# Layer 1's foreign-position mask: from an addition on VectorE to an 8-row matmul on TensorE

## The chip, the cores and the metric

The kernel runs on one core of one Trainium2 chip. Its engines are TensorE (PE, with its weight loads as PEld), VectorE (DVE), ScalarE (ACT), GpSimd (POOL) and SyncE (SP), which issues DMAs. The metric is device time in microseconds; the median of several runs is compared.

## What is computed

The reference is a two-layer transformer on x of shape [4, 512, 256]. The change lies in layer 1's attention, which attends over the first axis of 4, for each of 512 positions by itself:

```python
def _L1_attn_ref(x, w_qkv, w_proj):                 # x: (s=4, b=512, 256)
    s, b, _ = x.shape
    qkv = jnp.einsum('sbh,ph->sbp', x, w_qkv)
    ...                                             # 16 query heads, 4 key/value heads, head size 128
    scores = jnp.einsum('bhsd,bhtd->bhst', q, k) * scale
    attn = jax.nn.softmax(scores, axis=-1)          # over t, four values
    out = jnp.einsum('bhst,bhtd->bhsd', attn, v)
    ...
    return jnp.einsum('sbe,he->sbh', out, w_proj)

x = x + _L0_attn_ref(_layernorm(x), ...)
x = x + _L0_ffn_ref(_layernorm(x), ...)
x = x + _L1_attn_ref(_layernorm(x), L1_attn_w_qkv, L1_attn_w_proj)
x = x + _L1_ffn_ref(_layernorm(x), ...)
```

So each position has, for each head, a 4 x 4 matrix of scores.

## The kernel before

Four stages follow each other, one for each line above. In stage 3, `layer1_attention`, the 512 positions are split in G = 4 rounds of 128. A round's 512 rows of X (4 sequence items times 128 positions) are normalised, transposed on TensorE (`turn`), and multiplied by the weights into 20 tiles of queries and keys (`queries_keys`, 16 query heads and 4 keys, 128x512 each). ScalarE rounds a tile to bf16 (`qk_hi`), and VectorE makes the rest (`qk_lo`); all products are formed as high*high + high*low + low*high.

`scores` takes the round in NB = 4 blocks j, one PSUM bank each. A block holds four groups of 8 positions. The 8 positions and 4 sequence items of a group are the 32 keys of one column tile of TensorE, and the same 32 are the queries, for all heads. Of the 32 x 32 products of a head only those between equal positions are wanted: 4 of 32 in a row. The others, those of foreign positions, get a mask of -1e30. Before the change VectorE does it: `softmax_a(g, j)` transposes the bank in 32x32 blocks to SBUF, adds `mask` (128x32, broadcast over the heads), takes the maximum over the 8 positions (which leaves one value for each of the 4 items), then the maximum of the four, and subtracts. ScalarE takes the exponential, and `softmax_b` sums, inverts, multiplies, spreads the four weights over 32 columns with `same` (128x8, 1 at equal positions), and transposes back. `outputs` multiplies with the values, `project` applies the output projection and adds to X.

The orders are written out by hand and are the same for each round. TensorE: values(g), turn(g+1), five chunks of four tiles of queries_keys(g+1) with outputs(g, 0) to (g, 3) behind the first four chunks, project(g, 0), scores(g+1), project(g, 1). VectorE: normalised and x_low for g+1; then phases with softmax_b(g, 0) and softmax_a(g, 2); softmax_b(g, 1), outputs_lo(g, 0) and softmax_a(g, 3); softmax_b(g, 2) and outputs_lo(g, 1); and so on, each followed by three decoding steps for the weights of stage 4 and mixed evenly with four qk_lo (`interleave`, which spreads extra steps over a given number of main steps); at the end add(g, 0), softmax_a(g+1, 0) and (g+1, 1), add(g, 1). ScalarE: qk_hi of a chunk, outputs_hi, an exponential. In the last round there are no tiles to be made.

GpSimd first builds `mask` (16 dependent affine_selects, lines 1345 to 1349) and `same` (line 1352), and after them computes rstd of the layer norm (lines 1355, 1357), for which `normalised(0)` waits. Later it turns decoded 4-bit weights into bf16 pairs: line 154 (multiplication by scales), 157 (cast), 159 (rest), released by the last decoding step on VectorE, line 141.

Lines in the rows below: 1370 all three-product matmuls, 1381 the transposes `turn`, 1419 scores, 1436 outputs; on VectorE 1536 to 1551 softmax_a (1539 is the mask's addition), 1557 to 1575 softmax_b, 1582 outputs_lo, 1589 qk_lo, 1606 normalised, 1631 the addition to X; on ScalarE 1484 qk_hi, 1490 the value copies, 1496 the exponential, 1502 outputs_hi.

## Time and profile before

| what | value |
|---|---|
| median of 3 runs | 1284.75 us (1284.47 to 1284.92) |
| the profiled execution | 1279.96 us |
| its span | 1278.20 us |
| mean granted TensorE clock | 0.894 |
| TensorE matmuls busy | 1028.5 us, 80% |
| VectorE busy | 871.9 us, 68% |
| ScalarE busy | 499.3 us, 39% |
| GpSimd busy | 334.7 us, 26% |

Stage 3 runs from 642.8 us to about 985 us of the span. Its rounds 0 to 2 are nearly alike, 81 us each; the last is shorter. In the timeline a row gives start, duration, engine, line, operation, output<-inputs, and in square brackets how long the engine had been idle before and what ended that. Durations on TensorE contain the passage through the array, and the rows of neighbouring matmuls overlap: the distance from start to start is the pace. A row with xN merges N instructions.

### The profile page before, as it was taken

To read this page: it belongs to the slowest core of one execution; us is meant where nothing else is said; L and a number is where in the kernel's file an instruction comes from. 1 tells how busy PE (TensorE), PEld (TensorE's weight loads), DVE (VectorE), ACT (ScalarE), POOL (GpSimd) and SP (SyncE) were. 2 spreads that over 40 slices of the span, in tenths; PEclk is the share of its full clock that TensorE was granted. 3 is DMA by queue.
4 is the path that set the end of the run, shared out by engine and by line. 5 is a ranking of instruction groups with operands and counts; after the bars stand their busy time and mean duration, and the time that the engine had idled before them with its cause. 6 is when DMAs were issued, how large, how long until landed. Compare 5 with 4: busy or idle time off the path is not lost. (4 is left out here: it accounts for less than half of the span.)

```text
span 1278.2 us, 20287 instructions
## 1 busy us (share of the span) xinstructions
PE 1028.5 (80%) x6960; PEld 592.4 (46%) x6960; DVE 871.9 (68%) x1548; ACT 499.3 (39%) x972; POOL 334.7 (26%) x347
## 2 busy tenths in 40 slices
PE   2898888965859679497358998989968799999996
PEld 1444444533435345253124464464647355556553
DVE  4776667623789989989855845627572587777764
ACT  1144444442645544546323413414220244444442
POOL 2042424252343425342410311302131350000000
PEclk9698999997879789698669899898988899999998
DMA  6422121101001001001000000100000110000001
GB/s 172 93 76 84 54 92 47 51 3 39 1 1 41 1 1 41 0 1 42 1 16 2 26 10 9 25 2 18 15 17 1 41 27 1 1 1 0 1 1 66
DMA packets 37017, 35.78 MB, mean 28 GB/s; under 512 B 8520, under 2 KB 33352, under 8 KB 36944
## 3 DMA queue, kind: packets, MB, share of 16 engines
q1 hardware_dynamic: 35664, 33.79, 9.6%
q10 hardware_dynamic: 1280, 1.05, 0.6%
q8 instruction: 42, 0.69, 0.2%
q14 instruction: 31, 0.25, 0.1%
HBM read 27.28 MB, written 6.29 MB: 26 GB/s over the span
## 5 line engine op out<-in xcount | busy, mean ns | idle before, releaser
L779 DVE TENSOR_REDUCE bm<-ps 128x4 f32<-128x512 f32 x160 | 106.2, 685 | 36.5 <-PE ps L549 32.0
L696 ACT ACTIVATE pt<-ps 128x1024 f32<-128x1024 f32 (+1 forms) x96 | 82.3, 881 | 79.3 <-PE ps L603 78.0
L967 POOL TENSOR_TENSOR wt<-lg,mid 128x2048 f32<-128x2048 f32 x16 | 74.7, 4670 | 84.2 <-DVE mid L1186 84.2
L993 PE MATMUL ps<-stage,ones 128*128 128x512 bf16 x128 | 52.5, 410 | 54.7 <-DVE xr_lo L1152 26.3
L545 PE MATMUL ps<-ks,qs 96*128 96x512 bf16 (+3 forms) x256 | 71.3, 324 | 22.4 <-DVE bm L779 8.6
L1589 DVE TENSOR_TENSOR qk_lo<-ps,qk_hi 128x512 bf16<-128x512 f32 x80 | 54.8, 685 | 42.2 <-ACT qk_hi L1484 41.7
L1801 ACT ACTIVATE g<-ps 128x512 f32<-128x512 f32 x64 | 38.2, 597 | 111.9 <-PE ps L1748 111.9
L1851 DVE SCALAR_TENSOR_TENSOR g<-g,ps 128x512 f32<-128x512 f32 x64 | 43.9, 686 | 53.8 <-ACT g L1801 53.5
L493 POOL TENSOR_SCALAR_AFFINE_SELECT pt<-pt 128x256 f32<-128x256 f32 (+1 forms) x96 | 45.9, 482 | 128.4 <-ACT pt L696 128.0
L1209 DVE SCALAR_TENSOR_TENSOR X<-ps,cw,X 128x256 f32<-128x256 f32 (+1 forms) x128 | 61.9, 484 | 23.0 <-PE ps L997 14.8
L1763 PE MATMUL ps<-ew_hi,it_hi 128*128 128x256 bf16 x256 | 70.0, 273 | 7.8 <-DVE it_lo L1867 5.1
L1484 ACT ACTIVATE qk_hi<-ps 128x512 bf16<-128x512 f32 x80 | 47.8, 598 | 72.6 <-PE ps L1370 72.6
L1370 PE MATMUL ps<-xT_hi,wq_hi 128*128 128x512 bf16 x160 | 70.0, 437 | 7.7 <-DVE xT_lo L1612 5.0
L1370 PE MATMUL ps<-wp_hi,oT_hi 128*128 128x256 bf16 x256 | 71.0, 277 | 4.9 <-DVE oT_lo L1582 4.9
L154 POOL TENSOR_TENSOR mag_gu<-stage 128x512 f32<-128x512 fp8e4 x16 | 17.6, 1098 | 214.8 <-DVE stage L141 214.8
L1098 ACT ACTIVATE far<-far 128x256 f32<-128x256 f32 x128 | 51.4, 406 | 50.4 <-DVE far L1198 50.4
L1370 PE MATMUL ps<-wp_lo,oT_hi 128*128 128x256 bf16 x256 | 71.0, 277 | 0.0
L1370 PE MATMUL ps<-wp_hi,oT_lo 128*128 128x256 bf16 x256 | 71.0, 277 | 0.0
L1763 PE MATMUL ps<-ew_hi,it_lo 128*128 128x256 bf16 x256 | 70.0, 273 | 0.0
L1763 PE MATMUL ps<-ew_lo,it_hi 128*128 128x256 bf16 x256 | 69.9, 273 | 0.0
L1370 PE MATMUL ps<-xT_lo,wq_hi 128*128 128x512 bf16 x160 | 69.4, 434 | 0.0
L1370 PE MATMUL ps<-xT_hi,wq_lo 128*128 128x512 bf16 x160 | 68.6, 429 | 0.0
(228 smaller groups left out, 2826.1 us busy)
## 6 DMA issues: line engine op xcount, KB each, us to landing
qs<-scratch_q SPq DMA_DIRECT2D x64, 64.0 KB, 2.6
ks<-scratch_k SPq DMA_DIRECT2D x48, 64.0 KB, 2.5
q_next<-in_w_qkv SPq DMA_DIRECT2D x4, 768.0 KB, 4.8
X<-in_x SPq DMA_DIRECT2D x4, 512.0 KB, 7.0
w_next<-in_router_w SPq DMA_DIRECT2D x4, 512.0 KB, 4.1
w_next<-in_expert_w SPq DMA_DIRECT2D x4, 512.0 KB, 5.0
p_next<-in_w_proj SPq DMA_DIRECT2D x4, 512.0 KB, 5.6
out<-X SPq DMA_DIRECT2D x4, 512.0 KB, 4.7
```

The source lines that it names most:

```text
L493: pool.affine_select(out=t, in_=t, compare_op=ALU.is_ge, fill=0.0, base=0, pattern=[[0, len(heads)], [1, P]], channel_multiplier=-1).then_ ...
L545: pe.matmul(ps[:, o + P * i:o + P * (i + w)], qs[0:SHIFT, h, P * j:P * (j + 1)], ks[0:SHIFT, h, P * k0:P * (k0 + w)], start=(i == 0), stop ...
L696: act.activation(pt[kt][:, heads[0]:heads[-1] + 1, :], src, ACT.Exp).then_inc(s_exp, 1)
L779: ins = dve.tensor_reduce(bm[:, 2 * g + i // 5, 4 * (i % 5):4 * (i % 5) + 4], src.rearrange("p (k q) -> p k q", k=4), AX_X, ALU.max)
L967: pool.tensor_tensor(wt[:, :, :], lg[t % 2][:, :, :], over_experts(mid), ALU.subtract).then_inc(s_mid, 1)
L993: pe.matmul(out, ones4[:, :], bias, start=True, stop=False)
L1098: act.activation(far[:, e, :], far[:, e, :], ACT.Copy, accum_out=cw[t % 2][:, e:e + 1]).then_inc(s_cw, 1)
L1209: dve.scalar_tensor_tensor(x, bank(4 + u, D, D * e), c_t[:, 2 * u + e:2 * u + e + 1], x, ALU.mult, ALU.add).then_inc(s_c, 1)
L1370: mm = pe.matmul(out, lhs[a](c), rhs[b_](c), start=(n == 0), stop=(n == 3 * chunks - 1), **kw)
L1484: act.activation(qk_hi[:, m // (HQ + 1), m % (HQ + 1), :], bank(QK_BANK[m]), ACT.Copy).then_inc(s_qkhi, 1)
L1589: dve.tensor_tensor(qk_lo[:, k, h, :], bank(QK_BANK[m]), qk_hi[:, k, h, :], ALU.subtract).then_inc(s_qklo, 1)
L1763: mm = pe.matmul(bank(6 + t // 2, D, D * (t % 2)), a[m % 2][:, P * t:P * (t + 1)], w[2][:, m % 2, D * (m // 2):D * (m // 2 + 1)], start=(m ...
```

## The change

The mask goes into PSUM ahead of the scores. For each bank j, TensorE first issues one matmul of spread8 (8 rows x 128, bf16, 1 where column mod 8 is the row) with apart (8 rows x 512, bf16, 0 where column mod 8 is the row and -1e30 elsewhere), over the full bank, with start=True. The scores of the bank are then added with start=False. There are 4 such matmuls in a scores call, 16 in all. VectorE's addition is gone in each of the 16 softmax_a, whose steps are 4 instead of 5, and the counts of `interleave` follow. GpSimd builds `same` directly (128x8 instead of 128x32), and apart and spread8 from it, still ahead of rstd. TensorE waits for both before scores(0).

```diff
-        SMA, SMB = 5, 5
-        TURNED, MASKED, PICKED, MAXED, SHIFTED = 1, 2, 3, 4, SMA
+        SMA, SMB = 4, 5
+        TURNED, PICKED, MAXED, SHIFTED = 1, 2, 3, SMA
...
-                pool.memset(mask[:, :], -1.0e30).then_inc(const, 1)
+                pool.memset(same[:, :], 0.0).then_inc(const, 1)
                 for m in range(P // 8):
                     pool.wait_ge(const, 2 + m)
-                    mk = mask[:, :].rearrange("p (b q) -> p b q", q=8)
-                    pool.affine_select(out=mk, in_=mk, compare_op=ALU.not_equal, fill=0.0, base=-8 * m,
-                                       pattern=[[0, 4], [-1, 8]], channel_multiplier=1).then_inc(const, 1)
+                    pool.affine_select(out=same[:, :], in_=same[:, :], compare_op=ALU.not_equal, fill=1.0, base=-8 * m,
+                                       pattern=[[-1, 8]], channel_multiplier=1).then_inc(const, 1)
                 pool.wait_ge(const, 2 + P // 8)
-                pool.tensor_scalar(same[:, :], mask[:, 0:8], 0.0, None, ALU.is_ge).then_inc(const, 1)
+                pool.tensor_scalar(apart[:, :].rearrange("p (n q) -> p n q", q=8),
+                                   same[:, :].rearrange("p (o q) -> p o q", o=1).to_broadcast([P, BANK // 8, 8]),
+                                   1.0e30, -1.0e30, ALU.mult, ALU.add).then_inc(const, 1)
+                pool.tensor_copy(spread8[0:8, :].rearrange("p (n q) -> p n q", q=8),
+                                 same[0:8, :].rearrange("p (o q) -> p o q", o=1).to_broadcast([8, P // 8, 8])
+                                 ).then_inc(const, 1)
...
                     for j in range(NB):
+                        pe.matmul(bank(j), spread8[0:8, :], apart[0:8, :], start=True, stop=False, skip_group_check=True)
                         for k in range(KV):
...
-                                        start=(i == 0), stop=(i == 2), skip_group_check=True)
+                                        start=False, stop=(i == 2), skip_group_check=True)
...
+                pe.wait_ge(const, 4 + P // 8)
                 scores(0)
...
-                    dve.tensor_tensor(s[:, :, :], s[:, :, :],
-                                      mask[:, :].rearrange("p (o q) -> p o q", o=1).to_broadcast([P, H1, T8]),
-                                      ALU.add).then_inc(s_sma, 1)
-                    yield
-                    dve.wait_ge(s_sma, SMA * n + MASKED)
```

On GpSimd, at the head of stage 3, there stood before:

```order
L1344 MEMSET half 128x16
L1345 MEMSET mask 128x32
L1349 AFFINE_SELECT mask<-mask 128x32 x16
L1352 TENSOR_SCALAR same<-mask 128x8
L1355 TENSOR_SCALAR rstd<-mv 128x4
L1357 TENSOR_TENSOR rstd<-rstd,half 128x4
```

and now:

```order
L1345 MEMSET half 128x16
L1346 MEMSET same 128x8
L1349 AFFINE_SELECT same<-same 128x8 x16
L1352 TENSOR_SCALAR apart<-same 128x512
L1355 CAST spread<-same 8x128
L1360 TENSOR_SCALAR rstd<-mv 128x4
L1362 TENSOR_TENSOR rstd<-rstd,half 128x4
```

One operation more, of 512 columns, stands ahead of rstd.

On TensorE, at the start of scores(0), behind the last tile of queries and keys, there stood before:

```order
L1370 MATMUL ps<-xT_hi,wq_hi 128x512
L1370 MATMUL ps<-xT_lo,wq_hi 128x512
L1370 MATMUL ps<-xT_hi,wq_lo 128x512
L1419 MATMUL ps<-qk_hi 32x128 x4
L1419 MATMUL ps<-qk_lo,qk_hi 32x128 x4
L1419 MATMUL ps<-qk_hi,qk_lo 32x128 x4
```

and now:

```order
L1375 MATMUL ps<-xT_hi,wq_hi 128x512
L1375 MATMUL ps<-xT_lo,wq_hi 128x512
L1375 MATMUL ps<-xT_hi,wq_lo 128x512
L1420 MATMUL ps<-apart,spread 128x512
L1425 MATMUL ps<-qk_hi 32x128 x4
L1425 MATMUL ps<-qk_lo,qk_hi 32x128 x4
L1425 MATMUL ps<-qk_hi,qk_lo 32x128 x4
```

The mask matmul stands ahead of the twelve fours of its bank; at banks 1 to 3 it has fours on both sides.

On VectorE, in the first phase of a round, from softmax_a(g, 2) to the decoding steps (stage) and the first step of softmax_b(g, 1), with the tiles (qk_lo) between them, there stood before:

```order
L1536 STREAM_TRANSPOSE ew_hi<-ps 128x512 [waits softmax1,sc1]
L1539 TENSOR_TENSOR ew_hi<-ew_hi,mask 128x512 [waits shifted1]
L1589 TENSOR_TENSOR qk_lo<-ps,qk_hi 128x512 [waits qk1hi]
L1544 TENSOR_REDUCE four<-ew_hi 128x64 [waits shifted1]
L1548 TENSOR_REDUCE mx_0<-four 128x16 [waits shifted1]
L1551 TENSOR_TENSOR four<-four,mx_0 128x64 [waits shifted1]
L1589 TENSOR_TENSOR qk_lo<-ps,qk_hi 128x512 [waits qk1hi]
L135 TENSOR_SCALAR stage<-stage 128x64 [waits gathered_gu]
L138 TENSOR_SCALAR stage<-stage 128x128 [waits decoded_gu]
L141 SCALAR_TENSOR_TENSOR stage<-stage 128x128 [waits decoded_gu]
L1557 TENSOR_REDUCE sm_1<-four 128x16 [waits exp1]
L1589 TENSOR_TENSOR qk_lo<-ps,qk_hi 128x512 [waits qk1hi]
```

and now:

```order
L1543 STREAM_TRANSPOSE ew_hi<-ps 128x512 [waits softmax1,sc1]
L1546 TENSOR_REDUCE four<-ew_hi 128x64 [waits shifted1]
L1591 TENSOR_TENSOR qk_lo<-ps,qk_hi 128x512 [waits qk1hi]
L1550 TENSOR_REDUCE mx_0<-four 128x16 [waits shifted1]
L1553 TENSOR_TENSOR four<-four,mx_0 128x64 [waits shifted1]
L135 TENSOR_SCALAR stage<-stage 128x64 [waits gathered_gu]
L1591 TENSOR_TENSOR qk_lo<-ps,qk_hi 128x512 [waits qk1hi]
L138 TENSOR_SCALAR stage<-stage 128x128 [waits decoded_gu]
L141 SCALAR_TENSOR_TENSOR stage<-stage 128x128 [waits decoded_gu]
L1559 TENSOR_REDUCE sm_1<-four 128x16 [waits exp1]
L1591 TENSOR_TENSOR qk_lo<-ps,qk_hi 128x512 [waits qk1hi]
```

The addition is gone, the tiles stand at the same step numbers and so one step of the softmax later, and the last tile shown (tile 4) keeps its place behind L1557's step.

## Rows read from the trace of the kernel before

**Rows 1.** Waits, 680 to 965 us: engine line <- waited for: total us, times, longest.

```profile
DVE X L1631 <- PE ps L1370: 53.6, 6, 10.2
...
PE ps L1436 <- DVE oT_lo L1582: 18.1, 12, 5.3
```

**Rows 2.** Groups of instructions: the mask's addition, busy us, mean ns of one.

```profile
L1539 DVE TENSOR_TENSOR ew_hi<-ew_hi,mask 128x512 f32<-128x512 f32 x8 | 5.5, 693 | 0.3
```

**Rows 3.** Timeline, VectorE, the border between rounds 0 and 1.

```profile
771.36 0.69 DVE L1631 TENSOR_TENSOR X<-ps,X 128x512 f32<-128x512 f32 x1 [8.50 <-PE ps L1370]
```

**Rows 4.** Timeline, TensorE: the end of scores(1), and a change of shape in round 1.

```profile
760.44 0.24 PE L1419 MATMUL ps<-qk_lo,qk_hi 128*32 128x128 bf16 x4
760.50 0.24 PE L1419 MATMUL ps<-qk_hi,qk_lo 128*32 128x128 bf16 x4
760.67 0.28 PE L1370 MATMUL ps<-wp_hi,oT_hi 128*128 128x256 bf16 x1
...
786.57 0.38 PE L1370 MATMUL ps<-xT_lo,wq_hi 128*128 128x512 bf16 x1
786.79 0.38 PE L1370 MATMUL ps<-xT_hi,wq_lo 128*128 128x512 bf16 x1
787.10 0.39 PE L1436 MATMUL ps<-ew_hi,v 32*128 32x128 f32 x4
```

**Rows 5.** Timeline, GpSimd and VectorE, the start of stage 3.

```profile
647.80 0.25 POOL L1352 TENSOR_SCALAR same<-mask 128x8 f32<-128x8 f32 x1
...
649.49 1.38 DVE L1606 TENSOR_SCALAR xn<-X,mv,rstd 128x256 f32<-128x256 f32 x4 [4.95 <-POOL rstd L1357]
```

**Rows 6.** Groups of instructions on GpSimd, by form: busy us, mean ns of one.

```profile
L949 POOL TENSOR_SCALAR ties<-identb 128x128 bf16<-128x128 bf16 x8 | 4.2, 530 | 0.6
...
L1349 POOL TENSOR_SCALAR_AFFINE_SELECT mask<-mask 128x32 f32<-128x32 f32 x16 | 3.7, 229 | 1.1
...
L457 POOL CAST b_part<-b_next 2x512 bf16<-2x512 f32 x4 | 2.4, 599 | 0.0
...
L1935 POOL TENSOR_SCALAR_AFFINE_SELECT ident<-ident 128x128 f32<-128x128 f32 x1 | 0.3, 292 | 0.2 <-POOL ident L1933 0.2
```

**Rows 7.** Timeline, TensorE, values(0), turn(1), the first tile, and turn(2).

```profile
692.47 0.38 PE L1370 MATMUL ps<-wq_hi,xT_lo 128*128 128x512 bf16 x1
695.33 1.07 PE L1381 MATMUL ps<-ident,xn 128*128 128x128 f32 x8 [2.49 <-ACT v L1490]
698.02 0.59 PE L1370 MATMUL ps<-xT_hi,wq_hi 128*128 128x512 bf16 x1 [1.62 <-ACT xT_hi L1477]
...
778.25 1.06 PE L1381 MATMUL ps<-ident,xn 128*128 128x128 f32 x8 [0.78 <-ACT v L1490]
```

**Rows 8.** Timeline, ScalarE and VectorE, round 0, tile 4.

```profile
708.56 1.24 ACT L1484 ACTIVATE qk_hi<-ps 128x512 bf16<-128x512 f32 x2
...
709.21 0.69 DVE L1589 TENSOR_TENSOR qk_lo<-ps,qk_hi 128x512 bf16<-128x512 f32 x1
```

**Rows 9.** Timeline, VectorE and GpSimd, round 0, tiles 8 and 9.

```profile
720.27 0.69 DVE L1589 TENSOR_TENSOR qk_lo<-ps,qk_hi 128x512 bf16<-128x512 f32 x1 [1.00 <-ACT qk_hi L1484]
...
721.16 0.23 DVE L1563 TENSOR_TENSOR four<-four,sm 128x64 f32<-128x64 f32 x1
...
721.42 0.69 DVE L1567 TENSOR_TENSOR ew_hi<-four,same 128x512 f32<-128x512 f32 x1
721.47 1.65 POOL L159 TENSOR_TENSOR up_lo<-mag_gu,up_hi 128x512 bf16<-128x512 f32 x1 [0.18 <-POOL up_hi L157]
...
722.45 0.69 DVE L1589 TENSOR_TENSOR qk_lo<-ps,qk_hi 128x512 bf16<-128x512 f32 x1 [0.34 <-ACT qk_hi L1484]
```

**Rows 10.** Timeline, GpSimd and VectorE, the last round.

```profile
940.83 1.10 POOL L154 TENSOR_TENSOR mag_gu<-stage 128x512 f32<-128x512 fp8e4 x1 [34.51 <-DVE stage L141]
941.00 1.00 DVE L1563 TENSOR_TENSOR four<-four,sm 128x64 f32<-128x64 f32 x1
...
943.38 1.15 POOL L159 TENSOR_TENSOR gate_lo<-mag_gu,gate_hi 128x512 bf16<-128x512 f32 x1 [0.18 <-POOL gate_hi L157]
```

More of the change, by code:

```diff
@@ L1266, in layer1_attention @@
         v = st.sb("v1", [P, NB, KV, HD1], F32)
-        mask = st.sb("mask1", [P, T8], F32)
         same = st.sb("same1", [P, 8], F32)
+        apart = st.sb("apart1", [P, H1 // KV * T8 * KV], BF16)
+        spread8 = st.sb("spread8", [P, P], BF16)
         mx = [st.sb(f"mx1_{n}", [P, H1], F32) for n in range(2)]
@@ L1621, in _ @@
                 x_low(0)
-                dve.wait_ge(const, 3 + P // 8)
+                dve.wait_ge(const, 2 + P // 8)
                 interleave(queries_keys_low(0), NM, chain(statistics(1), statistics(2), statistics(3)), 6 * B)
```

## The prediction

> **What bounds the kernel now.** I read three views of layer 1's attention, in this order: the waits of its stretch, the timeline of a border between two rounds, and the timeline inside a round. In the waits the reader is to see that each engine waits for the other. VectorE waits 53.6 us for TensorE before the additions to X; TensorE waits 18.1 us for VectorE before the attention outputs, inside the rounds [rows 1]. So the path changes engine by place, and the change has to be weighed place by place. It takes 16 additions of 0.69 us from VectorE (8 on ew_hi [rows 2], 8 alike on ew_lo), 0.73 each with the gap, and gives TensorE 16 matmuls.
>
> **The three borders between rounds.** Two of a round's additions stand here, in softmax_a(g+1, 0) and (g+1, 1). Behind them VectorE idles 8.50 us until project(g, 1) is done [rows 3]; they are hidden, and taking them away gains 0. TensorE has no slack: project(g, 0), scores(g+1) and project(g, 1) follow without a gap, and X, the values and the next transposes hang on the last of them. What scores(g+1) grows by is paid in full.
>
> No 8-row matmul stands in the trace, so its price comes from neighbours. A 512-column matmul followed by one of another array shape leads to the next start 0.31 us later (786.79 to 787.10), against 0.22 in the same shape (786.57 to 786.79) [rows 4]. The column-tiled 128*32 matmuls run in fours, 0.06 us from four to four, but the first full-width one starts 0.17 behind the last four (760.50 to 760.67) [rows 4]: going from them into the mask matmul costs 0.11 more. At banks 1 to 3 that makes 0.31 + 0.11 = 0.42 us; at bank 0 the change of shape on the way in is paid today already, so 0.31. One scores call grows by 0.31 + 3 x 0.42 = 1.57 us, the three borders by **4.7 us**. Lower bound: 12 x 0.22 = 2.6. Upper bound, nothing overlaps: the 0.24 of a four's own row less its 0.06, and the 0.38 of a 512-column row [rows 4], 0.56 each, 12 x 0.56 = 6.7. I take 0.42 and 0.31, since both parts are measured changes of shape in this stage.
>
> The Trainium skill, TensorEngine Tiling (Array Packing), Key Properties, says that changing the tiling mode drains TensorE. This speaks against the change, since the mask matmul is put between column-tiled ones, two changes a bank. A full drain would make the borders 6.7 instead of 4.7. The trace agrees only in part: the full-width matmul starts 0.17 us after the four's start, while the four's row lasts 0.24 [rows 4].
>
> **The start of the stage.** GpSimd builds its constants before rstd, and VectorE waits 4.95 us for that rstd [rows 5], with TensorE behind. GpSimd's order is the path. Its 16 affine_selects shrink from 32 to 8 columns: 0.229 at 32 and 0.292 at 128 [rows 6] are 0.66 ns a column, so 16 x 24 columns save 0.25. The comparison of 0.25 (128x8) goes [rows 5], and the copy spread8 (8x128) comes; I take it at the same 0.25. The tensor_scalar apart has 512 columns: 0.53 at 128 [rows 6] and 0.25 at 8 [rows 5] are 2.33 ns a column, so 1.42. Sum -0.25 - 0.25 + 0.25 + 1.42 = **+1.2 us**, all on the path. Lower bound: the 512-column cast's 0.60 instead of 1.42 [rows 6], +0.4. I take 1.42, by the rows of the same operation.
>
> **Round 0.** scores(0) grows by 1.57 too. But turn(1) now starts at 695.33, 2.49 us after the values' end, behind ScalarE's four value copies [rows 7]; those come behind exp(0, 1), which waits for softmax_a(0, 1). Two additions less bring them forward by 1.46, and then the end of the values decides: 692.47 + 0.38 + 1.57 = 694.42, and the transposes 0.78 behind, as in round 1 (778.25) [rows 7], at 695.20: **-0.1 us**. The wait before turn(1) falls from 2.49 to 0.8, which may spare half-rate matmuls after it; I count nothing for that (rival e).
>
> **Inside rounds 0 to 2.** Two additions each, in softmax_a(g, 2) and (g, 3). The first is followed by three decode steps, a step of softmax_b and then qk_lo of tile 4. This starts at 709.21, right behind ScalarE's qk_hi of it (708.56, two rows of 0.62, the first done near 709.2) [rows 8]. ScalarE is late because outputs_hi(g, 0) stands ahead in its queue, and that hangs on TensorE. VectorE arrives 0.8 us earlier and waits 0.8 longer. Behind the second addition VectorE already waits 1.00 us for tile 8 at 720.27 [rows 9]. Gain in six places: 0; what is late next is ScalarE, behind TensorE.
>
> There is a loss. VectorE's multiplication L1563 lasts 0.23 us [rows 9], but 1.00 where GpSimd's L154 runs: it then ends 0.07 after L154's 941.93 [rows 10]. Two operations that both read two SBUF tensors do not overlap here. GpSimd's chain L154, L157, L159 is released by the decode steps. In phase 2 these move 0.7 us forward, while L1563 stays at 721.16, behind tile 8. L159 now starts at 721.47 behind L1567's 721.42 and lasts 1.65 [rows 9]; moved to 720.75 it goes first and takes its usual 1.15 [rows 10], until 721.90. L1563 then ends at 721.98 and L1567 at 722.70, 0.6 later than now. VectorE's wait of 0.34 us before tile 9 [rows 9] takes a part: tile 9 and the oT_lo behind it, for which TensorE waits, come 0.2 us later, and 0.3 and 0.4 in rounds 1 and 2, where I read that wait as 0.28 and 0.18. **+0.9 us** together. In phase 1 the same shift puts L1567 about 0.05 us ahead of L159; I count nothing.
>
> **The last round.** No tiles are made, and VectorE's queue is the path: TensorE's longest wait for it, 5.3 us [rows 1], is here. Both additions count, except that after the first oT_lo meets an oT_hi that is not ready: 0.54 + 0.73 = **-1.3 us**.
>
> **Sum.** 4.7 + 1.2 - 0.1 + 0.9 - 1.3 = +5.4 us. The profiled execution took 1279.96 us (span 1278.20 and 1.76 around it): 1285.4. It lies 4.8 below the median of the timed runs, and nothing shown says where; I assume the same offset after the change and add the difference to the median: 1284.75 + 5.4 = **1290.1 us**, +0.42%.
>
> **Rivals.**
> (a) Faster: VectorE is the path inside the rounds after all, six additions of 0.73 pay -4.4 in place of the +0.9, and the mask matmuls cost 0.22. Sum 2.6 + 1.2 - 0.1 - 4.4 - 1.3 = -2.0, 1282.7; it stays below the time before up to 0.38 us a mask matmul. For it: the 18.1 us of waits [rows 1]. Against: each addition is followed by a VectorE wait for ScalarE.
> (b) The additions to both queues are cheap, 0.22 a matmul and 0.4 at the start: 2.6 + 0.4 - 0.1 + 0.9 - 1.3 = +2.5, 1287.2. For it: no row has an 8-row operand. Against: the changes of shape in rows 4.
> (c) Full drain: 6.7 in place of 4.7, +7.4, 1292.1.
> (d) In phase 1 L159 comes first and L1567 waits 1.1 us for it, in three rounds: +8.7, 1293.5. For it: a margin of 0.05. Against: VectorE won with the same margin at 721.42 [rows 9].
> (e) TensorE's clock. At 698.02 a 512-column matmul takes 0.59 us instead of 0.38 [rows 7], the pace of 1.2 instead of 2.4 GHz, after TensorE had idled. Five such matmuls more or fewer are 1.1 us of either sign. This widens the cases and is none by itself.
>
> **Chances.** Forecast 0.55, (a) 0.07, (b) 0.18, (c) 0.10, (d) 0.10. A measurement can tell about 0.2% (2.6 us) from no change. Slower by more: 0.76 (forecast, c, d, a little of b); within: 0.19 (most of b, a part of a); faster: 0.05, with a clock gain on (a). The range leaves out (a) and the upper part of (d): from 1285.8, (b) with a clock gain, to 1294.5, (d) with a clock loss.
>
> **What would show it.** From the first matmul of scores(g+1) to project(g, 1): 1.6 us more. The operation apart at 1.4 us on GpSimd and rstd 1.2 later. VectorE's wait before tile 8 at 1.7 instead of 1.0 us, with tile 8 as far behind ScalarE as now. L1563 of phase 3 at 0.8 instead of 0.23. The last round's final outputs nearer to its values by 1.3. The forecast is wrong if tiles 4 and 8 follow VectorE's step before them without a wait, or if a mask matmul takes under 0.3 us from start to start.

## The result

Each of the two kernels was timed 12 times: 1283.61 us median before and 1286.22 us after, a ratio of 1.0029 with a 95% interval of 1.0015 to 1.0042. The ratio compares the means; the medians lie 2.6 us apart, the means 3.7 us. The change makes the kernel slower, by about 3.7 us. Timed a second time, beside other runs of the kernel before, the same kernel stood at 1.0042 (1.0026 to 1.0058), 5.4 us (after_again below). The forecast was +5.4 us, +0.42%.

The profiled execution of the kernel after took 1288.49 us, its span 1286.8 us, 8.6 more than the span before. Not all of this is the change: in this trace stage 3 starts at 647.74 us instead of 642.78, before any changed instruction has run. In the second profile of the same kernel it starts at 642.60. So the stage is compared from its own start on.

The first view of the profile after is the busy time of the engines.

```profile
PE 1036.8 (81%) x6976; PEld 599.3 (47%) x6976; DVE 862.3 (67%) x1532; ACT 499.7 (39%) x972; POOL 334.4 (26%) x348
```

16 matmuls more on PE, 16 instructions less on DVE (1532 against 1548) and 9.6 us less busy there. These answer to [rows 1], waits of stage 3 from 680 us to its end (engine line <- waited for: total us, times, longest):

```profile
DVE X L1633 <- PE ps L1375: 60.9, 6, 10.4
...
PE ps L1442 <- DVE oT_lo L1584: 20.4, 16, 4.2
```

VectorE waits 7.3 us longer for TensorE at the borders, and TensorE's wait for oT_lo has not fallen (20.4 against 18.1), though VectorE has less to do. Two things lengthen the wait at the borders: the additions that used to fill a part of it are gone, and scores last longer. How much is due to which was not separated.

The window view gives a stretch's start and end, its length, the busy time of PE, PEld, DVE, ACT and POOL (with counts), the granted TensorE clock and the DMA's share. Three stretches of the kernel before: stage start to the first transposes, scores at the second border, outputs(3, 0) to project of the last round.

```profile
642.78:650.93 8.15, 0.00 (x0) 0.00 (x0) 3.11 (x12) 0.00 (x0) 5.31 (x21) 0.50 0.31 60
838.62:841.41 2.79, 2.79 (x193) 2.69 (x193) 2.42 (x4) 0.00 (x0) 0.00 (x0) 1.00 0.02 6
941.04:965.31 24.27, 11.65 (x129) 9.61 (x129) 21.83 (x43) 8.53 (x18) 13.73 (x15) 0.61 0.10 23
```

The same of the kernel after:

```profile
647.74:657.23 9.49, 0.00 (x1) 0.01 (x1) 3.11 (x12) 0.00 (x0) 5.38 (x22) 0.50 0.24 55
843.74:848.14 4.40, 4.40 (x197) 3.08 (x196) 3.63 (x7) 0.26 (x1) 0.00 (x0) 1.00 0.01 4
950.51:973.56 23.05, 12.09 (x128) 10.04 (x129) 20.54 (x42) 8.54 (x18) 13.03 (x15) 0.60 0.09 24
```

Three terms of the forecast can be read off: the start is 1.34 longer (forecast 1.2), a scores call 1.61 (1.57), the last round 1.22 shorter (1.3). What lies between is less plain, and most experiments are about it.

### The profile page after: what moved, and what is told of

The parts are those of the page before. It is cut to its first block and busy times, and to the rows that moved or that the text cites. A ratio compares the mean times of both kernels' runs of the same rounds, so it can differ in the third digit from the quotient of the medians.

```text
span 1286.8 us, 20309 instructions
## 1 busy us (share of the span) xinstructions
PE 1036.8 (81%) x6976; PEld 599.3 (47%) x6976; DVE 862.3 (67%) x1532; ACT 499.7 (39%) x972; POOL 334.4 (26%) x348
## 3 DMA queue, kind: packets, MB, share of 16 engines
q10 hardware_dynamic: 1280, 1.05, 0.6%
## 5 line engine op out<-in xcount | busy, mean ns | idle before, releaser
L154 POOL TENSOR_TENSOR mag_gu<-stage 128x512 f32<-128x512 fp8e4 x16 | 17.6, 1099 | 217.5 <-DVE stage L141 217.5
L1375 PE MATMUL ps<-xT_hi,wq_hi 128*128 128x512 bf16 x160 | 66.9, 418 | 8.2 <-DVE xT_lo L1614 5.0
L995 PE MATMUL ps<-rw_hi,xr_hi 128*128 128x512 f32 x128 | 69.6, 544 | 0.0
L1375 PE MATMUL ps<-xT_lo,wq_hi 128*128 128x512 bf16 x160 | 66.1, 413 | 0.0
```

The lines of the kernel that those rows point to most:

```text
L995: pe.matmul(out, x_hi(c), w_hi[:, c, cols], start=False, stop=False)
L1375: mm = pe.matmul(out, lhs[a](c), rhs[b_](c), start=(n == 0), stop=(n == 3 * chunks - 1), **kw)
```

## The experiments

All ratios are to the kernel before, timed on the same chip. A profile of each kernel was taken too. mask_128 and wide_select were timed once each, for their profiles; they have no ratio.

### The two halves of the change, one at a time

The first kernel takes the additions away and puts nothing in their place. Its output is not the reference's.

```diff
-                    dve.tensor_tensor(s[:, :, :], s[:, :, :],
-                                      mask[:, :].rearrange("p (o q) -> p o q", o=1).to_broadcast([P, H1, T8]),
-                                      ALU.add).then_inc(s_sma, 1)
```

> The kernel before without its 16 additions and with no mask matmul: layer 1's foreign positions are not masked out, a part of the computation is left out. It shows what the additions were worth to the kernel before, with scores and start unchanged. Theory of the prediction: the last round 1.3, round 0's start about 1.6 less what the values' end leaves of it, inside the rounds nothing or a loss of 0.9: 1 to 2.5 us faster than the kernel before. Rival, VectorE as the path inside: 1.3 + 1.5 + 4.4 = 7 us faster.

The second keeps both, the mask matmuls and the additions; its small constant for them is made after rstd.

```diff
+                    if n == 0:
+                        pool.tensor_scalar(mask[:, :].rearrange("p (n q) -> p n q", q=8),
+                                           same[:, :].rearrange("p (o q) -> p o q", o=1).to_broadcast([P, T8 // 8, 8]),
+                                           1.0e30, -1.0e30, ALU.mult, ALU.add).then_inc(const, 1)
...
+                    dve.tensor_tensor(s[:, :, :], s[:, :, :],
+                                      mask[:, :].rearrange("p (o q) -> p o q", o=1).to_broadcast([P, H1, T8]),
+                                      ALU.add).then_inc(s_sma, 1)
```

> The changed kernel with VectorE's 16 additions kept as well (the mask is then put on twice); their 128x32 mask is built by GpSimd after round 0's rstd. It shows what the additions are worth where the matmuls are there. Theory of the prediction: only the last round's two count, 1.3 us, and the 0.9 us of collisions inside the rounds go away: 0.4 us slower than the changed kernel, 1286.6. Rival, VectorE as the path inside the rounds: 6 x 0.73 + 1.3 = 5.7 us slower, 1292. In between, if the second addition of a round counts wherever TensorE runs at full rate (as in rounds 0 and 1 of the changed kernel's profile): 0.7 to 0.9 for each such round, 2 to 3.5 us slower.

| | no mask matmuls | mask matmuls |
|---|---|---|
| with additions | 1 (before) | 1.0039 (1.0024 to 1.0055) |
| without additions | 0.9988 (0.9967 to 1.0010) | 1.0029 and 1.0042 (after, twice) |

Read along the lower row, mask matmuls and their constants cost 0.41 to 0.54%, 5 to 7 us; the terms of the forecast on that side (borders 4.7, start 1.2, scores(0) 1.57) make 7.5. Read down the columns, the additions are worth 0.12% without mask matmuls, and -0.03 or +0.10% with them: 1.5 us at most by the middle values, with intervals of 0.15 to 0.2% to either side, so not told apart from nothing. Sixteen additions of 0.73 us are 11.7 us of VectorE's time. Most of it was hidden, or given back elsewhere.

The traces say where they count. The last round is 23.05 us in no_mask and 24.29 in keep_add: 1.2 us, as forecast. The other place is round 0: from scores(0) to turn(1) no_mask takes 9.19 us, where before takes 10.63. The two additions are worth 1.44 us there, as the forecast had it (1.46), and the four mask matmuls of scores(0) use that up. What they do inside the rounds is told below.

### The matmul itself: its rows, and its place

One kernel makes it 128 rows tall, with zeros in the other 120 rows of `spread8`.

```diff
-                        pe.matmul(bank(j), spread8[0:8, :], apart[0:8, :], start=True, stop=False, skip_group_check=True)
+                        pe.matmul(bank(j), spread8[:, :], apart[:, :], start=True, stop=False, skip_group_check=True)
```

> The changed kernel with the mask matmul over all 128 rows (rows 8 to 127 of spread8 are zero): twelve times the contraction rows, the same 512 columns, and at bank 0 no change of shape on the way in. If the price is that of columns and of the change from and to the column-tiled fours, the distance from one mask matmul of a call to the next stays at 1.10 us. If the few rows are what makes it dear or cheap, it moves. One memset more at the start, 0.2 to 0.3 us.

Another puts the four mask matmuls together ahead of the call's scores, so that there is one change of shape in place of seven.

```diff
                     for j in range(NB):
                         pe.matmul(bank(j), spread8[0:8, :], apart[0:8, :], start=True, stop=False, skip_group_check=True)
+                    for j in range(NB):
                         for k in range(KV):
```

> The changed kernel, with the four mask matmuls of a scores call issued together ahead of all the scores, so that the array's shape changes once instead of four times. If about half of a mask matmul's 0.43 us is the change of shape, the four cost 0.22 each and one change of 0.1: a scores call falls from 4.70 us (761.87 to 766.57) to about 4.0, and the three borders by 2 us together, 1284.3. If the 512 columns with 8 rows are dear in themselves, the call stays at 4.6 to 4.7.

The second border in the window view, first of mask_128, then of masks_first:

```profile
839.25:843.67 4.42, 4.42 (x198) 3.01 (x196) 3.66 (x7) 0.26 (x1) 0.00 (x0) 1.00 0.01 4
```

```profile
844.40:848.16 3.76, 3.76 (x198) 2.98 (x197) 2.38 (x5) 0.00 (x0) 0.00 (x0) 1.00 0.02 4
```

120 rows more (16 times the rows; the expectation's "twelve times" is a slip) cost 0.02 us a call, nothing. The order does count: without a mask a call takes 2.79, with the four together 3.76, with them apart 4.40. So the columns of the four cost 0.97, about 0.24 each, and the changes of shape between the banks 0.64, 0.21 for each of the three banks. The forecast had 0.22 and 0.20 (0.31 + 0.11 - 0.22).

The timeline of the kernel after shows it matmul by matmul:

```profile
762.81 0.23 PE L1425 MATMUL ps<-qk_hi,qk_lo 128*32 128x128 bf16 x4
762.97 0.38 PE L1420 MATMUL ps<-apart,spread 8*128 8x512 bf16 x1
763.29 0.24 PE L1425 MATMUL ps<-qk_hi 128*32 128x128 bf16 x4
...
764.07 0.39 PE L1420 MATMUL ps<-apart,spread 8*128 8x512 bf16 x1
764.39 0.24 PE L1425 MATMUL ps<-qk_hi 128*32 128x128 bf16 x4
```

From the last four to the mask matmul 0.16 us (0.06 without a change), from it to the next four 0.32 (0.22). Sum above the pace of fours: 0.42, the number of the forecast. A full drain would have cost 0.56 by the lengths of the rows; here neither change waits for the 0.23 or 0.38 us that its forerunner's row lasts (the profile models the ends of these rows, so this compares with modelled ends).

In the time of the kernel the better order shows nothing: 1.0039 (1.0024 to 1.0053) for masks_first, beside 1.0029 and 1.0042. Two borders save 0.64 each, but the first of that profile has a stall, "[1.46 <-issue]" 0.6 us before the call's end, told of below, and the interior of round 0 came out long (43.08 us, at a granted clock of 0.80). A gain of some 2 us in 1280 isn't settled by these runs.

### GpSimd's constants, off the path

GpSimd builds the constants between the first rstd and the second instead of ahead of both. In the kernel after (`apart` and `spread8` move with the selects):

```diff
-                pool.memset(same[:, :], 0.0).then_inc(const, 1)
-                for m in range(P // 8):
...
                 for n, rows in enumerate((slice(0, 1), slice(1, G))):
+                    if n == 1:
+                        pool.memset(same[:, :], 0.0).then_inc(const, 1)
+                        for m in range(P // 8):
...
                     wait_alone(pool, s_mv, B * rows.stop, passed_pool)
```

> The changed kernel, with GpSimd's 16 affine_selects, apart and spread8 moved behind round 0's rstd. In the changed kernel rstd starts 6.6 us after the stage's first GpSimd instruction and VectorE waits 6.28 us for it, though its statistics end 1.7 us after that instruction. If GpSimd's order is the path at the stage's start, VectorE's wait falls to about 1.5 us (0.2 + 0.2 + 1.04 of rstd), the kernel is 4.8 us faster than the changed one, about 1281.5, and 1 to 2 us faster than the kernel before; the constants are ready long before scores(0). If something else stands behind (a weight or a DMA), the gain is under 1 us.

The stage reaches its first transposes 4.88 us after its start instead of 9.49, and the ratio falls from 1.0029 and 1.0042 to 1.0015 (0.9996 to 1.0033). That is 1.8 to 3.5 us by the middle values, less than the 4.6 us saved at the start, and the kernel did not come out faster than the kernel before, as had been expected. The part of the forecast on round 0 can be read here without a half-rate stretch: scores(0) to turn(1), before and in this kernel.

```profile
684.70:695.33 10.63, 8.15 (x216) 4.98 (x217) 6.31 (x15) 2.98 (x7) 2.90 (x3) 1.00 0.01 2
```

```profile
679.88:690.40 10.52, 9.74 (x220) 5.35 (x221) 4.90 (x12) 3.11 (x7) 2.91 (x3) 1.00 0.01 2
```

-0.11 us, with PE 1.59 us busier: the two additions less pay for the four matmuls more, as the forecast had it (-0.1).

The same move in the kernel before, with its `mask` and `same`:

> The kernel before with mask and same built behind round 0's rstd, VectorE's additions kept, no mask matmul. If GpSimd's order is the path at the stage's start there as well, the stretch from the stage's first GpSimd instruction to the first transposes falls from 8.15 to 4.9 us and nothing else moves: 3.3 us faster than the kernel before, ratio 0.9975, and faster than both kernels. If the earlier start is given back at the half rate of TensorE's clock, under 2 us.

It gave 0.9971 (0.9956 to 0.9987), 3.7 us less than before: faster than both kernels, and close to the 3.3 us expected. Its first transposes come 4.90 us after the stage's start instead of 8.15, and the whole stage, to the first transposes of the next, takes 348.64 us instead of 352.14. 

Late constants and mask matmuls together:

> The changed kernel with both edits: constants behind round 0's rstd, and the four mask matmuls of a scores call together. By sections against the kernel before: -3.3 at the start, three scores calls +0.96 each, the last round -1.2, round 0 -0.1, inside the rounds -0.6 to +0.9 each: -1.7 us at the middle, ratio 0.9987. If it isn't below 1.000, something that the sections don't show takes the gain.

0.9985 (0.9969 to 1.0000), between the two and near the 0.9987 expected; its scores call takes 3.76 us at the second border, as in masks_first. With the constants out of the way, the mask on VectorE is still the better place than the mask matmuls of the change: 0.9971 against 1.0015 for late_const, with intervals that do not meet. Against the grouped ones (0.9985) the intervals overlap, and the runs do not settle it.

### The start of the stage, by its parts

The timeline of GpSimd at the head of stage 3, before, and after:

```profile
643.03 4.68 POOL L1349 TENSOR_SCALAR_AFFINE_SELECT mask<-mask 128x32 f32<-128x32 f32 x16
```

```profile
648.04 5.24 POOL L1349 TENSOR_SCALAR_AFFINE_SELECT same<-same 128x8 f32<-128x8 f32 x16
653.37 0.62 POOL L1352 TENSOR_SCALAR apart<-same 128x512 bf16<-128x512 f32 x1
654.05 0.28 POOL L1355 CAST spread<-same 8x128 bf16<-8x128 f32 x1
```

The sum of the forecast was right (+1.2, measured +1.34), but two of its parts were wrong and cancelled out. The operation apart takes 0.62 and not 1.42. The 16 selects got longer, by 0.56, where they should have saved 0.25. One kernel makes the tile wide again:

```diff
-                    pool.affine_select(out=same[:, :], in_=same[:, :], compare_op=ALU.not_equal, fill=1.0, base=-8 * m,
-                                       pattern=[[-1, 8]], channel_multiplier=1).then_inc(const, 1)
+                    pool.affine_select(out=wd, in_=wd, compare_op=ALU.not_equal, fill=1.0, base=-8 * m,
+                                       pattern=[[0, 4], [-1, 8]], channel_multiplier=1).then_inc(const, 1)
```

> The kernel after, with the 16 affine_selects made over 128x32 again, as in the kernel before, and `same` taken from the first 8 columns; all else as after. If the time of a dependent step on GpSimd grows when the tile gets narrower (0.293 us at 32 columns against 0.328 at 8, as the two traces have it), the 16 selects take 4.7 us instead of 5.24 and the stage's first transposes come 0.5 us earlier. If instead the slower steps come from elsewhere (the order of the instructions around them, or the state of that run), they stay at 5.2.

```profile
645.61 5.85 POOL L1351 TENSOR_SCALAR_AFFINE_SELECT wide<-wide 128x32 f32<-128x32 f32 x16
```

The theory that narrower steps take longer fell: wide is slower still. But the groups by form tell more (busy us, mean ns of one | idle time just before them), here of the kernels before and after and of wide_select:

```profile
L1349 POOL TENSOR_SCALAR_AFFINE_SELECT mask<-mask 128x32 f32<-128x32 f32 x16 | 3.7, 229 | 1.1
```

```profile
L1349 POOL TENSOR_SCALAR_AFFINE_SELECT same<-same 128x8 f32<-128x8 f32 x16 | 3.1, 193 | 2.3
```

```profile
L1351 POOL TENSOR_SCALAR_AFFINE_SELECT wide<-wide 128x32 f32<-128x32 f32 x16 | 3.7, 231 | 2.3
```

The duration does go by the width (229 and 231 ns at 32 columns, 193 at 8); what doubled is the idle time between the steps, from 1.1 to 2.3 us, in both kernels that fill in 1.0 in place of 0.0. The last kernel goes back to starting from -1e30 and filling in 0.0, in the narrow tile, with a comparison behind it:

```diff
-                pool.memset(same[:, :], 0.0).then_inc(const, 1)
+                pool.memset(mask8[:, :], -1.0e30).then_inc(const, 1)
...
-                    pool.affine_select(out=same[:, :], in_=same[:, :], compare_op=ALU.not_equal, fill=1.0, base=-8 * m,
+                    pool.affine_select(out=mask8[:, :], in_=mask8[:, :], compare_op=ALU.not_equal, fill=0.0, base=-8 * m,
...
+                pool.tensor_scalar(same[:, :], mask8[:, :], 0.0, None, ALU.is_ge).then_inc(const, 1)
```

> The kernel after, but its 16 affine_selects start from -1e30 and fill in 0.0, as those of the kernel before do, in the narrow 128x8 tile; a comparison (0.25 us, as before) then makes `same` of it. The wide select, back at 128x32, still had the longer gap: there 16 take 5.85 us at 231 ns each, where the kernel before takes 4.68 at 229; in the kernel after, 5.24 at 193. Theory: the gap between dependent steps is 0.07 us with fill 0.0 and 0.14 with fill 1.0. Then the 16 take 16 x (0.193 + 0.07) = 4.2 us, the comparison gives back 0.25 to 0.35, and turn(0) comes 0.7 us earlier than in the kernel after: 8.8 instead of 9.49 us behind the stage's start. Rival: the gap comes from where the tile lies or from what stands around the selects; they stay at 5.2 us and turn(0) comes 0.3 us later. In the time of the kernel 0.7 us are 0.05%, at the edge of what the rounds can tell: expected ratio 1.003.

```profile
643.58 4.09 POOL L1350 TENSOR_SCALAR_AFFINE_SELECT mask<-mask 128x8 f32<-128x8 f32 x16
647.76 0.25 POOL L1353 TENSOR_SCALAR same<-mask 128x8 f32<-128x8 f32 x1
```

```profile
L1350 POOL TENSOR_SCALAR_AFFINE_SELECT mask<-mask 128x8 f32<-128x8 f32 x16 | 3.1, 192 | 1.1
```

4.09 us, and the idle time is 1.1 again. The fill value, or the value that stands in the tile, which was changed along with it, makes 0.07 us a step; which of the two was not tried. turn(0) comes 8.59 us after the stage's start instead of 9.49. The time of the kernel doesn't show the 0.9: 1.0039 (1.0023 to 1.0056). In the profile of that run scores(0) to turn(1) takes 13.59 us at a granted 0.75, against 12.02 at 0.86 in the kernel after, which alone is more than what the start gained.

### Inside the rounds: the collision and the clock

The forecast gave the interiors +0.9 us for one mechanism: GpSimd's L159, released earlier, meets VectorE's multiplication (L1565 after, L1563 before). Here is round 2 of the kernel after, VectorE and GpSimd:

```profile
889.78 0.69 DVE L1591 TENSOR_TENSOR qk_lo<-ps,qk_hi 128x512 bf16<-128x512 f32 x1 [1.59 <-ACT qk_hi L1491]
...
890.66 1.09 DVE L1565 TENSOR_TENSOR four<-four,sm 128x64 f32<-128x64 f32 x1
...
890.52 1.16 POOL L159 TENSOR_TENSOR up_lo<-mag_gu,up_hi 128x512 f32 x1 [0.25 <-POOL up_hi L157]
```

The wait before tile 8 has grown from 1.00 to 1.59 (forecast 1.7), L159 takes 1.16 instead of 1.65, and the multiplication ends 0.07 behind it, 1.09 us long instead of 0.23. In rounds 0 and 1 of this trace the picture is another: TensorE was granted its full clock (1.00, the 2.4 GHz) there, ScalarE's tile 8 came early, and the multiplication met the end of L154, 0.54 and 0.53 us long. Tile 8 followed VectorE's step before it there without a wait, which the forecast had named as a sign that it is wrong; in the third round, and in all three of the second profile, the wait was there (1.59, then 0.91, 1.60 and 1.04 us). The stretch in question, from the first matmul of outputs(g, 1) to that of outputs(g, 2), in round 0 of before, and in rounds 0 and 2 of after:

```profile
713.16:724.48 11.32, 11.05 (x56) 5.54 (x57) 9.74 (x22) 4.06 (x9) 3.77 (x5) 0.70 0.10 28
```

```profile
719.15:728.66 9.51, 7.91 (x56) 4.11 (x57) 9.27 (x21) 4.48 (x9) 3.50 (x4) 1.00 0.10 27
...
882.67:894.50 11.83, 10.86 (x56) 5.63 (x57) 10.00 (x21) 4.59 (x9) 3.21 (x4) 0.71 0.10 27
```

At the same granted clock (0.70, 0.71) the stretch is 0.5 us longer without the addition (11.83 against 11.32). At 1.00 it is 9.5, against 10.11 in the one round of keep_add that was granted 1.00. So at the full clock VectorE is the bound (busy 9.27 of 9.51) and the addition does count, 0.6 us; where half-rate matmuls are among them TensorE is (11.05 of 11.32), and the collision is what remains. Which of them a round gets is not the addition's doing alone: one and the same kernel got 1.00, 1.00 and 0.71 in one profile and 0.83, 0.71, 0.84 in the other.

The last two edits move phase 2's three decoding steps ahead of softmax_a(g, 3), so that L159 is through before the multiplication comes.

```diff
-                            (chain(softmax_b(g, 1), outputs_lo(g, 0), softmax_a(g, 3)), SMB + OC + SMA),
+                            (chain(softmax_b(g, 1), outputs_lo(g, 0), dq.decode(dve, NU2 * g + 1, 1), softmax_a(g, 3)), SMB + OC + SMA),
...
-                        interleave(chain(main, dq.decode(dve, NU2 * g + i, i % 2)), steps + DEC, tiles, 0 if last else QK)
+                        if i != 1:
+                            main = chain(main, dq.decode(dve, NU2 * g + i, i % 2))
+                        interleave(main, steps + DEC, tiles, 0 if last else QK)
```

In the kernel after, and in the kernel before with late constants:

> The kernel after, with one part of VectorE's order moved: in phase 2 of a round the three decoding steps stand ahead of softmax_a(g, 3) instead of behind it, so that GpSimd's rest of the weights (L159) is released about 2.8 us earlier and is through before softmax_b's multiplication (L1565) comes. Theory (the collision costs): in the round whose outputs(g, 2) run at the half rate, L1565 falls from 1.09 to 0.23 us and outputs(g, 2) from 11.83 to about 11.2; in the last round the multiplication behind the moved steps falls from 1.00 too; the kernel gains 1 to 2 us on the kernel after, ratio to before about 1.0015 to 1.003. Rival (the collision is hidden by another wait, TensorE's own pace or ScalarE's): L1565 gets short but outputs(g, 2) keeps its 11.8 in a half-rate round and its 9.5 at full rate, and the ratio stays at 1.003 to 1.004. Second rival: the collision only moves to another pair (L154 or L159 with an L1565 of the phase before), and the number of long L1565 stays the same.

> The kernel before with the constants built behind round 0's rstd (as in before_late, 0.9971) and with phase 2's decoding steps ahead of softmax_a(g, 3). Theory (collision on the path in the last round only, there 0.77 us for one long multiplication): 0.5 to 1 us below before_late, ratio 0.9962 to 0.9968. Rival (nothing of it on the path, or the earlier L154 meets another multiplication): 0.997 as before_late. If the ratio is above 0.998, moving the decoding steps ahead of the maxima delays the exponential and costs more than the collision.

In decode_early the multiplication of phase 3 takes 0.22 or 0.23 us in each of rounds 0 to 2. The interiors of rounds 0 to 2, from the first matmul of outputs(g, 0) to that of project(g, 0), in the window view; four blocks: before, after, the second profile of after, and decode_early:

```profile
705.30:746.11 40.81, 36.55 (x226) 17.78 (x225) 32.53 (x70) 18.57 (x35) 13.79 (x16) 0.83 0.12 27
787.10:828.03 40.93, 36.64 (x225) 17.82 (x225) 32.56 (x70) 18.57 (x35) 13.62 (x16) 0.83 0.13 27
869.23:910.06 40.83, 36.54 (x225) 17.90 (x225) 32.51 (x70) 18.57 (x35) 13.63 (x16) 0.83 0.10 26
```

```profile
711.33:751.28 39.95, 34.53 (x225) 17.43 (x224) 31.16 (x68) 18.47 (x35) 13.55 (x16) 0.87 0.11 28
793.00:833.15 40.15, 34.59 (x225) 17.41 (x224) 31.22 (x68) 18.47 (x35) 13.66 (x16) 0.87 0.10 27
874.69:917.92 43.23, 37.83 (x225) 19.45 (x225) 31.88 (x68) 18.58 (x35) 13.23 (x16) 0.80 0.09 24
```

```profile
707.37:748.86 41.49, 36.43 (x226) 18.42 (x225) 30.99 (x68) 18.58 (x35) 13.54 (x16) 0.84 0.13 27
790.27:831.90 41.63, 36.52 (x226) 18.08 (x225) 31.89 (x68) 18.58 (x35) 13.23 (x16) 0.84 0.11 26
874.67:916.21 41.54, 36.24 (x226) 18.65 (x225) 30.96 (x68) 18.58 (x35) 13.66 (x16) 0.84 0.10 25
```

```profile
707.96:749.54 41.58, 36.04 (x225) 17.94 (x224) 30.97 (x68) 18.59 (x35) 13.06 (x16) 0.84 0.11 27
790.99:831.89 40.90, 36.51 (x225) 17.89 (x225) 31.01 (x68) 18.58 (x35) 13.23 (x16) 0.83 0.12 27
873.46:914.15 40.69, 36.30 (x226) 18.08 (x225) 30.91 (x68) 18.59 (x35) 13.24 (x16) 0.83 0.12 26
```

A round's length goes by the clock column first: without additions about 40.1 us at 0.87, 41.5 at 0.84, 43.2 at 0.80; with them 40.8 at 0.83, 41.5 at 0.84, and 40.10 and 40.65 in a round each of before_late and keep_add at 0.87. At one and the same clock the two kinds lie close together. The sums over the three rounds:

| kernels | interiors of rounds 0 to 2, us |
|---|---|
| with additions: before, keep_add, before_late | 122.57, 122.90, 122.35 |
| without: after, second profile, late_const, no_mask | 123.33, 124.66, 124.62, 123.51 |
| without: masks_first, late_masks_first, mask_128, zero_fill, wide_select | 124.88, 122.99, 125.92, 126.51, 126.13 |
| without, decoding early | 123.17 |
| with, constants late, decoding early | 123.80 |

The nine without additions (and with the old decoding order) have a mean of 124.7, the three with them 122.6. The interiors came out longer without the additions, by some 2 us in the mean; the lowest of the nine is 0.09 us above the highest of the three. The sign is that of the forecast, the size twice its 0.9. Not all of it is the collision: five of the 27 rounds without additions were at a granted 0.80 and took 43.1 to 43.4 us, none of the nine with them was, and the runs don't show whether the additions have to do with that.

To see the collision by itself, compare rounds with the same pattern of the clock: the stretch from outputs(g, 1) to outputs(g, 2) at a granted 0.69 to 0.71, and those behind it at 0.84 and 0.85. With additions there are seven, of before, keep_add, before_late and before_late_decode, of 40.7 to 41.0 us. Without them, and with a long multiplication (0.96 to 1.11 us), there are ten: one of 41.2 and nine of 41.5 to 41.8. Rounds 1 and 2 of decode_early have the pattern and a multiplication of 0.22 and 0.23: 40.90 and 40.69. The stretch itself, in round 1 of the second profile of after, then in rounds 1 and 2 of decode_early:

```profile
798.26:810.09 11.83, 11.07 (x57) 5.48 (x57) 9.99 (x21) 4.55 (x9) 3.20 (x4) 0.71 0.12 28
```

```profile
798.99:810.26 11.27, 10.99 (x56) 5.61 (x57) 9.02 (x21) 4.07 (x9) 3.21 (x4) 0.70 0.13 30
881.44:892.45 11.01, 10.85 (x56) 5.67 (x57) 9.03 (x21) 4.07 (x9) 3.21 (x4) 0.69 0.15 30
```

So in such a round the collision costs about 0.8 us, where the forecast had 0.2 to 0.4, and the earlier decoding gives it back. Round 0 of decode_early is the exception: its stretch takes 11.72 us at 0.71 with a multiplication of 0.23, as long as in round 0 of masks_first (11.70) with one of 0.96.

The ratio of decode_early, 1.0039 (1.0019 to 1.0059), shows no gain. Little was to be seen: 15 of the 27 rounds had a long multiplication, which makes 3 x 15/27 x 0.8 = 1.3 us as an estimate, 0.1%, and a part is lost again. The last round, where VectorE's queue is the path, is 23.38 us instead of 23.05, since the moved steps delay the maxima and the exponential behind them, and its three long multiplications (1.00, 0.88, 1.00) only moved.

In the kernel before there is no collision in phase 3 to be removed, and the move costs: 1.0008 (0.9996 to 1.0020) instead of 0.9971, interiors 1.45 us longer than in before_late, the last round 24.73 instead of 24.29. That one of its three long multiplications became short brought nothing. Its expectation had named delayed maxima as the reason should the ratio come above 0.998; the last round (0.44 us longer) fits that, and for the interiors it isn't shown, since they differ in the clock too.

## Why the prediction was right, and where it was not

Measured are the differences to the profile of before, in the two profiles of the kernel after.

| step | forecast, us | first profile | second profile |
|---|---|---|---|
| three borders | +4.7 | +3.9 | +3.6 |
| start of the stage | +1.2 | +1.3 | +1.3 |
| round 0, scores(0) to turn(1) | -0.1 | +1.4 | +1.4 |
| turn(g+1) to outputs(g, 0), rounds 0 and 2 | 0 | -2.6 | -0.1 |
| inside rounds 0 to 2 | +0.9 | +0.8 | +2.1 |
| last round | -1.3 | -1.2 | -1.2 |
| rest of the stage | 0 | 0.0 | -0.1 |
| sum | +5.4 | +3.6 | +7.0 |
| ratio | +0.42% | +0.29% (0.15 to 0.42) | +0.42% (0.26 to 0.58) |

The time went the way that was forecast and lies in the range. A part of that is luck: the start and the last round came out as forecast, but the other terms missed in both directions, by up to 2.6 us, and in part cancelled.

**The borders** carried the forecast, and the price of a matmul held: a call grew by 1.61 at the second border and 1.60 at the third. Both measured prices of a change of shape, 0.31 and 0.11 [rows 4], were taken from other pairs of shapes and were right for this one to 0.01 us. The first border of the pair grew by 0.72 only, because the kernel before has a stall there:

```profile
756.69:760.67 3.98, 2.98 (x193) 2.74 (x193) 3.62 (x7) 0.26 (x1) 0.00 (x0) 1.00 0.01 4
```

3.98 us, 1.00 of it some 0.5 us before the call's end, in which the profile shows nothing that TensorE waits for:

```profile
760.17 0.24 PE L1419 MATMUL ps<-qk_hi,qk_lo 128*32 128x128 bf16 x4 [1.00 <-issue]
```

I had read this border and taken its last rows [rows 4], and not seen it. It is no accident of one profile: all six profiles in which no mask matmul stands between the fours have such a stall (1.00 in before, 1.27 in no_mask, 1.19 in before_late and before_late_decode, 1.46 in masks_first, 1.27 in late_masks_first), and the eight with the mask matmuls apart have none above 0.22; there the call takes 4.40 to 4.81 us. So "follow without a gap" was wrong for the first border, where the mask matmuls take the place of idle time and the growth is 0.4 to 0.7 us instead of 1.6. What the stall is was not found.

The Trainium skill, TensorEngine Tiling (Array Packing), Key Properties, has a drain at each change of the tiling mode. The forecast took it as rival (c), with 1292.1 us as its time. The trace agrees in that each change costs something (0.10 us on either side). It doesn't bear out that the engine empties by the rows' own lengths, whose ends are modelled: that would have made it 0.56 a bank, and 0.42 was measured.

**The start** was right by cancellation. The step that missed is the extrapolation of apart from 128 and 8 columns of tensor_scalar, 2.33 ns a column: 512 columns took 0.62. The row that I had kept as the lower bound, the cast of 512 columns at 0.60 [rows 6], was the right neighbour. The other missed step is "0.66 ns a column saves 0.25" for the selects. The duration fell even more, by 16 x 0.036 = 0.6 us, but the time between the steps rose by 1.2 with the other fill value.

**Round 0.** The working was right: -0.11 us in late_const, at the full clock. In the kernel after, in both of its profiles, a half-rate stretch falls on scores(0), which lasts 5.89 us there and 4.39 in late_const. A stretch after turn(1) was gone in turn: from the first tile's start to outputs(0, 0) 6.01 us, against 7.28 before. The same gain stands before round 2, where turn(3) to outputs(2, 0) takes 8.86 us at a granted 1.00, against 10.14 at 0.83 before. In the second profile both gains were missing (7.25 and 10.10). The forecast had named this as (e) and counted nothing.

**Inside the rounds** the additions were hidden, as said: before tile 4 VectorE waits 0.93 us for ScalarE, where it had arrived just in time before [rows 8], and outputs(0, 1) is on time (7.82 against 7.86).

```profile
715.25 0.69 DVE L1591 TENSOR_TENSOR qk_lo<-ps,qk_hi 128x512 bf16<-128x512 f32 x1 [0.93 <-ACT qk_hi L1491]
```

So rival (a) falls in phase 1; in phase 2 it holds for the rounds at the full clock, 0.6 us each. Rival (d), a lost race in phase 1, falls too: the operation that spreads the weights (L1569, L1567 before) starts 0.32 us ahead of L159 in round 0 and 0.14 ahead in rounds 1 and 2, and takes its 0.69 us. The collision of phase 2 came as worked out (1.59 us of wait, 1.09 us of multiplication), in one round of three in either profile of the kernel after, and costs such a round about 0.8 us. What the forecast didn't have is the clock: a loss of 0.5 us for the stretch at a granted 0.71, a gain of 0.6 at 1.00, since each round before ran at 0.70 there.

**The total.** 1290.1 us was forecast and 1286.22 measured. 1.1 us of it is the base (before had 1283.61 over 12 runs, not 1284.75 over 3). The rest, in the ratio, is 0.42% against 0.29%, and the second timing gave 0.42%. It was rival (b) whose time, 1287.2, lay nearest, yet its mechanism, a matmul at 0.22 us, is not what the rows show.

What stays open: the cause of the stall, what decides where the half-rate stretches fall, and whether the time of the kernel has the gains that the traces show, 0.9 us less at the start (zero_fill), 0.64 us less in a scores call (masks_first) and 0.8 us less in a round with a collision (decode_early). Each is at or below what these intervals can tell, and the stage as a whole took 355.76 us in one profile and 359.12 in the other of the same kernel, with a granted clock of 0.88 and 0.87.

## What to carry to other kernels

Work that an engine does while it waits anyway is free, and moving it to the engine that is waited for costs its full price, even if it shrinks from 0.73 us to 0.42. Before adding a matmul of another shape between tiled ones, price the change of shape from the rows at hand (here 0.2 us a bank above its columns) and try to group such matmuls. Look first at what stands ahead of the first dependent result of a stage: 16 small constants on GpSimd were worth 3.7 us, as much as the question of where to put the mask.

## What the runs showed of the hardware

- A 512-column matmul of 8 rows and one of 128 rows cost the same here (4.40 and 4.42 us a call).
- Dependent affine_selects on GpSimd stand 0.07 us apart with fill 0.0 on -1e30 and 0.14 with fill 1.0 on 0.0, at 8 and at 32 columns alike (idle time 1.1 and 2.3 us before 16 of them).
- A multiplication of 128x64 on VectorE takes 0.23 us alone and up to 1.11 (no_mask) beside a GpSimd operation that reads two SBUF tensors too. At the same granted clock the stretch with it was 0.5 us longer, and the round 0.8 us.
- The stall "issue" in the first border's scores is 1.00 to 1.46 us in the six profiles without a mask matmul between the fours, and at most 0.22 in the eight with them. Its cause was not found.
